# Two 384-column pieces of a selective scan joined into one of 768 columns

## The reference

```python
def step(h, xs_t):
    d_t, u_t, B_t, C_t = xs_t
    dA = jnp.exp(d_t[..., None] * A)
    h = h * dA + (d_t * u_t)[..., None] * B_t[:, :, None, :]
    y = jnp.einsum('bkdn,bkn->bkd', h, C_t)
    return (h, y)
...
x = x + _L0_conv_ref(_gn(x), ...)     # projections, 3x3 conv, the scans, gated output
x = x + _L1_conv_ref(_gn(x), ...)     # qkv, 3x3 conv, softmax(q k^T) v, projection
```

## Time and profile before

| | |
|---|---|
| time, median of 3 runs | 11736.53 us (11725.92 to 11742.42) |
| the profiled execution: its own time | 11744.59 us |
| the profiled execution: its span | 11742.8 us |
| DVE busy | 8777.8 us, 75% |
| PE busy (matmuls) | 7829.1 us, 67% |
| ACT busy | 6619.8 us, 56% |
| POOL busy | 5947.9 us, 51% |
| TensorE clock granted, mean | 0.763 of full |

### The profile page before, as it was taken

How to read it: one execution, slowest core, us unless ns; L and a number is a source line. 1 busy time by engine, 2 the same in 40 slices (tenths; PEclk the granted TensorE clock), 3 DMA queues, 4 the chain that set the end, 5 groups by cost and what they waited for, 6 DMA issues and landing times.

```text
span 11742.8 us, 196590 instructions
## 1 busy us (share of the span) xinstructions
PE 7829.1 (67%) x53104; PEld 2469.3 (21%) x53104; DVE 8777.8 (75%) x12459; ACT 6619.8 (56%) x12403; POOL 5947.9 (51%) x4844
## 2 busy tenths in 40 slices
PE   3555467873788638885487845878458774687758
PEld 1221122221222212221122211222112221222212
DVE  4998578975899649996499965989569986698740
ACT  3332366643676437763477634766257753576558
POOL 3665446644566336664266633666346654465420
PEclk7555578875888758886588866989568885798779
DMA  3554145531555225551355513554135541455310
GB/s 88 170 166 141 23 145 168 159 104 41 153 169 157 80 59 155 173 155 58 83 159 170 153 39 104 161 164 146 45 111 161 162 144 23 133 165 163 116 22 19
DMA packets 686888, 1411.01 MB, mean 120 GB/s; under 512 B 74400, under 2 KB 334272, under 8 KB 678080
## 3 DMA queue, kind: packets, MB, share of 16 engines
q1 hardware_dynamic: 686016, 1401.21, 40.0%
HBM read 1186.22 MB, written 214.70 MB: 119 GB/s over the span
## 4 chain that ended last, share of the span: by engine, by line
issue 34%; DVE 20%; POOL 19%; PE 15%; DMA 6%; ACT 4%; SPq 2%; DVEq 1%; POOLq 1%; ACTq 0%
POOL hc_buf L624 18%; DVE rings L980 11%; DVE ps L956 4%; PE ps L1347 3%; PE ps L1200 2%; DMA rep<-bc_scratch 2%; PE ps L1377 2%; PE ps L1378 2%; PE ps L1266 1%; ACT probs_buf L723 1%; DMA hc_buf<-y_scratch 1%; PE ps L1419 1%; POOL u_buf L295 1%; DVE rep L905 1%; DMA delta_scratch<-job_buf 1%
## 5 line engine op out<-in xcount | busy, mean ns | idle before, releaser
L624 POOL TENSOR_TENSOR hc_buf<-rings,rep 128x384 f32<-128x384 f32 x4608 | 4948.8, 1074 | 3713.1 <-DVE rings L980 3700.8
L723 ACT ACTIVATE probs_buf<-ps 128x384 f32<-128x384 f32 x6912 | 3081.3, 494 | 2008.1 <-PE ps L1266 1979.8
L956 DVE TENSOR_TENSOR ps<-ps,rep 128x384 f32<-128x384 f32 x4608 | 2505.8, 545 | 667.0 <-PE ps L1175 413.6
L1175 PE MATMUL ps<-st_buf,pick_channel 96*128 96x384 bf16 x4608 | 1722.7, 374 | 1531.8 <-DVE rings L980 1282.3
L1266 PE MATMUL ps<-qp_buf,kp_buf 108*128 108x384 bf16 (+1 forms) x6912 | 2224.8, 352 | 142.3 <-ACT job_buf L682 98.8
L980 DVE TENSOR_TENSOR_SCAN rings<-rings,ps 128x384 f32<-128x384 f32 x2304 | 2282.9, 991 | 9.0
L980 DVE TENSOR_TENSOR_SCAN rings<-st_buf,rings,ps 128x384 f32<-128x384 f32 x1920 | 1922.5, 1001 | 0.0
L1200 PE MATMUL ps<-probs_buf,v_buf 128*13 128x384 f32 x13824 | 1624.2, 545 | 31.8 <-ACT probs_buf L723 17.9
L1188 PE MATMUL ps<-hc_buf,sum_states 128*32 128x144 f32 x24576 | 1491.8, 330 | 86.8 <-POOL hc_buf L624 86.8
L714 ACT ACTIVATE st_buf<-st_buf,a_cols 128x768 f32<-128x768 f32 x1152 | 1076.7, 937 | 153.3 <-DMA st_buf<-delta_scratch 149.7
L1266 PEld LDWEIGHTS ps<-qp_buf,kp_buf 108*128 108x128 bf16 x6912 | 663.7, 98 | 2286.0 <-ACT probs_buf L723 1097.5
(11 more groups left out here) (147 smaller groups left out, 6751.2 us busy)
## 6 DMA issues: line engine op xcount, KB each, us to landing
st_buf<-delta_scratch SPq DMA_DIRECT2D x1152, 384.0 KB
rings<-delta_scratch SPq DMA_DIRECT2D x1152, 384.0 KB
part_scratch<-job_buf SPq DMA_DIRECT2D x1152, 72.0 KB, 2.8
st_buf<-part_scratch SPq DMA_DIRECT2D x192, 432.0 KB, 6.8
rep<-bc_scratch SPq DMA_DIRECT2D x192, 384.0 KB
delta_scratch<-job_buf SPq DMA_DIRECT2D x192, 192.0 KB, 5.2
qp_buf<-qk_scratch SPq DMA_DIRECT2D x864, 36.0 KB
kp_buf<-qk_scratch SPq DMA_DIRECT2D x432, 72.0 KB
```

What stands on the lines that cost most here:

```text
L624: pool.tensor_tensor(hc[tile % 2][:, cols], h_ring[x % 2], rep_piece(1, kk, v), ALU.mult)\
L723: act.activation(probs[(m % 2) * HG + h], bank(slots["score", p]), ACT.Exp, scale=SCALE)\
L956: dve.tensor_tensor(bu, bu, rep_piece(0, kk, v), ALU.mult)\
L1175: pe.matmul(bank(BANK_U[x % 3]), pick(x // 2), st[x // 2 // SPG][:, piece(v)], start=True, stop=True)\
```

## The change

A piece becomes a whole step of 768 columns for the broadcast, the product by B, the scan and the product by C, and the semaphores count steps in place of halves.

- PE writes a step's 768 columns with two matmuls (512 and 256 columns) into one of **two** u slots of two PSUM banks each (banks 2 to 5), one directly behind the other. Broadcast t waits for scan t-2.
- Scores, denominators, projection and jobs keep a ring of **two** banks in place of three.
- DVE's product t is followed directly by scan t, which reads it. The number of products and of scans goes from 4608 to 2304 each.
- `h_ring` becomes two slots of 768; the second lies in unused columns of `job_buf`.
- Delta loads, exp(delta A), sums over states, jobs and attention keep their size and their place. The part of attention without a scan beside it keeps its ring of 7.

```diff
-SCAN_RING = 3
+SCAN_RING = 2
...
-        h_ring = [rings[:, (6 + i) * PC:(7 + i) * PC] for i in range(2)]
+        h_ring = [rings[:, 6 * PC:8 * PC], job_buf[:, 8 * PC:10 * PC]]
...
-        BANK_U, BANK_Y, BANK_PV = (3, 4, 5), 6, 7
+        BANK_Y, BANK_PV = 6, 7
+        flat = ps[:, :, :].rearrange("p b c -> p (b c)")
+        U0 = 2 * 512
...
+        def u_slot(t, lo=0, hi=SC):
+            return flat[:, U0 + t % 2 * 1024 + lo:U0 + t % 2 * 1024 + hi]
...
-                            pool.tensor_tensor(hc[tile % 2][:, cols], h_ring[x % 2], rep_piece(1, kk, v), ALU.mult)\
-                                .then_inc(s["hc_ready"], 1)
+                            pool.tensor_tensor(hc[tile % 2][:, chunk(kk, v)], h_ring[t % 2], rep_third(1, kk, v),
+                                               ALU.mult).then_inc(s["hc_ready"], 1)
...
-                dve.wait_ge(s["ubc"], X + 1)
-                bu = bank(BANK_U[x % 3])
-                dve.tensor_tensor(bu, bu, rep_piece(0, kk, v), ALU.mult)\
+                dve.wait_ge(s["ubc"], kidx * DSTEPS + q * BODY + (t + 1))
+                dve.tensor_tensor(u_slot(t), u_slot(t), rep_third(0, kk, t % SPT), ALU.mult)\
                    .then_inc(s["b_ready"], 1)
...
-                if x % 2 == 0:
-                    dve.wait_ge(s["da_ready"], kidx * DSTEPS + q * BODY + (x // 2 + 1))
-                if not (first and x < 2):
+                dve.wait_ge(s["da_ready"], X + 1)
+                if not (first and t < 2):
 
                     dve.wait_ge(s["hc_ready"], X - 1)
-
-                if not (first and x == 0):
+                if not (first and t == 0):
                     dve.wait_ge(s["h_ready"], X)
                 dve.wait_ge(s["b_ready"], X + 1)
...
-                o, d0, d1 = h_ring[x % 2], da_ring[x // 2 % RD][:, piece(v % 2)], bank(BANK_U[x % 3])
+                o, d0, d1 = h_ring[t % 2], da_ring[t % RD], u_slot(t)
...
-                if scan:
-                    mult_b(kidx, kk, q, 0, first)
                 for t in range(BODY):
                     if scan:
-                        for x in (2 * t, 2 * t + 1):
-                            if x + 1 < 2 * BODY:
-                                mult_b(kidx, kk, q, x + 1, first)
-                            scan_half(kidx, kk, q, x, first)
+                        mult_b(kidx, kk, q, t, first)
+                        scan_chunk(kidx, kk, q, t, first)
...
-                if not (first and x < 3):
-                    pe.wait_ge(s["h_ready"], X - 2)
-                v = natural(kk, x % (2 * SPT))
-                pe.matmul(bank(BANK_U[x % 3]), pick(x // 2), st[x // 2 // SPG][:, piece(v)], start=True, stop=True)\
-                  .then_inc(s["ubc"], 1)
+                if not (first and t < 2):
+                    pe.wait_ge(s["h_ready"], X - 1)
+                src = st[t // SPG][:, chunk(kk, t % SPT)]
+                pe.matmul(u_slot(t, 0, 512), pick(t), src[:, 0:512], start=True, stop=True)
+                pe.matmul(u_slot(t, 512, SC), pick(t), src[:, 512:SC], start=True, stop=True).then_inc(s["ubc"], 1)
```

More of the change, by code:

```diff
@@ L305, in rep_third, with chunk @@
             return rep[:, slot * SC:(slot + 1) * SC]
-        def rep_piece(j, kk, v):
-            return rep_third(j, kk, v // 2)[:, piece(natural(kk, v) % 2)]
+        def chunk(kk, i):
+            cc = natural(kk, i)
+            return slice(cc * SC, (cc + 1) * SC)
+        def u_slot(t, lo=0, hi=SC):
+            return flat[:, U0 + t % 2 * 1024 + lo:U0 + t % 2 * 1024 + hi]
         loads = [(in_proj, "in_projT"), (taps[0], "taps_a"), (taps[1], "taps_b"),
@@ L612, in stretch @@
                     def stretch(q, first):
-                        for x in range(2 * BODY):
-                            X = kidx * (2 * DSTEPS) + q * (2 * BODY) + x
-                            tile, v = divmod(x, 2 * SPT)
-                            cols = piece(natural(kk, v))
-                            if first and tile == 0 and v % 2 == 0:
-                                pool.wait_ge(rep_loaded[v // 2], 32 * (kidx + 1))
+                        for t in range(BODY):
+                            X = kidx * DSTEPS + q * BODY + t
+                            tile, v = divmod(t, SPT)
+                            if first and tile == 0:
+                                pool.wait_ge(rep_loaded[v], 32 * (kidx + 1))
                             if v == 0 and not (first and tile < 2):
@@ L945, in job_stage, with mult_b, scan_chunk @@
                 ins.then_inc(s["job_dve"], 1)
[L947 to L956 removed]
+            def mult_b(kidx, kk, q, t, first):
+                if first and t < SPT:
+                    dve.wait_ge(rep_loaded[t], 32 * (kidx + 1))
+                dve.wait_ge(s["ubc"], kidx * DSTEPS + q * BODY + (t + 1))
+                dve.tensor_tensor(u_slot(t), u_slot(t), rep_third(0, kk, t % SPT), ALU.mult)\
                    .then_inc(s["b_ready"], 1)
[L959 to L961 removed]
+            def scan_chunk(kidx, kk, q, t, first):
+                X = kidx * DSTEPS + q * BODY + t
                 back = KS_ORDER[kk] >= 2
[L963 to L966 removed]
+                dve.wait_ge(s["da_ready"], X + 1)
+                if not (first and t < 2):
                     dve.wait_ge(s["hc_ready"], X - 1)
[L970 removed]
+                if not (first and t == 0):
                     dve.wait_ge(s["h_ready"], X)
@@ L973, in scan_half @@
                 init = 0.0
-                if x % (2 * SPT):
-                    prev = h_ring[(x + 1) % 2]
-                    init = prev[:, 0:1] if back else prev[:, PC - 1:PC]
-                o, d0, d1 = h_ring[x % 2], da_ring[x // 2 % RD][:, piece(v % 2)], bank(BANK_U[x % 3])
+                if t % SPT:
+                    prev = h_ring[(t + 1) % 2]
+                    init = prev[:, 0:1] if back else prev[:, SC - 1:SC]
+                o, d0, d1 = h_ring[t % 2], da_ring[t % RD], u_slot(t)
                 if back:
@@ L1287, in stretch @@
                     if scan:
-                        broadcast_u(kidx, kk, q, 2 * t, first)
+                        broadcast_u(kidx, kk, q, t, first)
                     if scan and t % SPT != 1:
@@ L1296, in stretch @@
                         score(PER_STEP * t + 1)
-                    if scan:
-                        broadcast_u(kidx, kk, q, 2 * t + 1, first)
                     if prev and t == DEN_MM:
```

30 lines of the change are left out of this document (11 added, 19 removed).

## The result

The changed kernel takes **12272.2 us** (median of 4 runs, 12261.58 to 12272.78) where the kernel before took 11735.42 us beside it (4 runs): a ratio of 1.0456, 95% interval 1.0438 to 1.0474. It is 537 us slower; 11654 us was forecast, range 11510 to 11860. The profiled execution's span is 12270.8 us, 528 us above that of before.

What follows compares the result with a forecast made beforehand. DVE was taken to set the pace wherever a scan runs. Terms +6 - 88 + 25 + 7 - 33 = -83 us from the profiled 11744.6 gave 11662, less 8 for the median: 11654 us, range 11510 to 11860.

Steps and rivals of the forecast that it cites:

- job products of over 2 us in every stretch (the port): Sign of being wrong: DVE job products lasting over 2 us in every stretch would show the port case.
- POOL, the port: DVE job products sometimes wait for POOL's longer C product at the shared port: 30 times 0.85 us, +25 us.
- the port rival: Four job products after a sum's copy, 72 stretches, all come behind the C product: 533 us, 12190 us; 6%.
- The joined step: DVE's 768-column product plus scan: 2.75 us against 2.74, scan's wait 0.09 us (bounds 0.04 to 0.16); +6 us.
- Waits for the broadcast: DVE's waits for PE's broadcast shrink by 12.6 us in each of 7 images with attention beside them: -88 us.
- step 8's wait: DVE's product of step 8 waits for the broadcast behind PE's projection; goes whole, some 6 us per image.
- Step 3's: Stall after the attention sum's copy, ended by ACT's exponential before step 3's scan; shrinks 0.56 us each, 5.6 us per image.
- End of a direction: Last sums wait for a C product ending 0.9 us later; B's load hides it in 24 of 32 directions: +7 us.
- The loop's branch: DVE stands 5.27 us behind a branch, 14 times; shorter loop body may end it: 0 to -67, taken -33 us.
- The ring of two: Rival: scores wait for exponentials, ACT falls behind, scans wait: up to 463 us, 12117 us, or 11886 in half the steps; 18%.
- The drain rule: Rival: DVE drains anyway, so a scan's wait for the product ahead costs nothing: 11260 us; 5%.
- Gains given back: Rival: stalls of steps 2 and 7 set by ACT's chain, branch stalls stay, port costs 25 us: 11736 us; 17%.

Runs made afterwards that it cites:

- e6: The kernel before, still 384-column pieces, with each scan directly behind its own product instead of the next piece's: 12839.62 us, ratio 1.094.
- e1: The kernel before with only POOL's C product widened to 768 columns, counting its semaphore by two: 11698.51 us, ratio 0.9979.
- e9: The kernel before with only the C product in 768 columns, as in e1, but counting its semaphore by one: 11695.8 us, ratio 0.9966.
- e4: The kernel before with a ring of two banks for scores, denominators, projection and jobs, nothing else: 11899.78 us, ratio 1.0156.
- e3: The changed kernel with every DVE job or leftover instruction of two SBUF inputs directly behind a scan, at most one per step: 11621.56 us, ratio 0.991.
- e11: The kernel before, C products in 384 columns, with only the new places of jobs and leftovers from e3: 11652.63 us, ratio 0.9922.
- e8: The changed kernel with each C product counting its semaphore by two instead of one, readers' waits doubled: 11863.06 us, ratio 1.0107.

## Why the prediction was wrong

The forecast's sum was -83 us; the same terms now, from the traces. The last sign of being wrong that the prediction names, "job products of over 2 us in every stretch (the port)", is the one that came.

- **POOL, the port: +25 us forecast, +639 measured.** This is the step that failed. The mechanism and its price were right: "Each would cost 0.85 us more" against 2.19 less 1.38 for one that was lost already, and 1.85 us against 1.65 to 1.85 for one newly lost. The count was not. I took the 30 of before as given, and gave the port rival 6% because "the order behind a scan's end is unchanged". It is unchanged, and so are the record starts, but what stands ahead of the scan is not: e6 turns the race by that alone. The rival had named four products per stretch at 72 stretches, 533 us; 404 are 5.6 per stretch, for it left out the second product of step 17 and the one behind the division.
- **The joined step: +6 us forecast, +133 measured.** The product's record is 0.95 us (forecast 0.94) and scan to next start 1.73 us (1.72, so two passes per column hold). The wait was mis-sized: 0.13 us, not 0.09. A step without extras is 2.805 us from scan to scan (steps 20 and 22) instead of 2.75, where before has 2.74; 2304 x 0.065 is 150 us, less the 17 us at the stretches' ends. It lies within the bounds that I had given. I had taken the wait of a scan for a scan; that of a product for a product was as near.
- **Waits for the broadcast: -88 us forecast; -152 measured for the broadcast and +81 for exp(delta A) behind it,** so -71. By steps: step 8's wait went whole, as forecast (33 us; forecast 42). Step 3's went from 163 to 64 us, but 78 us of waits of the scan, nearly all for exp(delta A), now stand in steps 2 to 5, so the stall that ACT's chain sets there shrank by 21 us where 39 were forecast. Scattered waits in other steps gave the rest. That -71 comes near -88 is partly luck.
- **The wait for B: not in the sum, -99 us.** e1 takes it to 141.6 us, e6 to 88.0: both the wide C product and the order on DVE shorten it. Part of it has only moved into the wait of the next line.
- **End of a direction: +7 us forecast, +44 measured** (128.4 less 84.5), the list has it in all 32 directions. e1, with the wide C product alone, has 116.5, so that product makes most of it; and as the wait for B behind it is 41 us shorter there, the load of B did hide most of it, as forecast.
- **The loop's branch: -33 us forecast, -67 measured.** The stall is gone from the list of waits. It stays in e6 (60.1 us) and e9 (64.8), whose loop bodies on DVE are as long as before, and in none of the runs with 768-column products. So neither the order nor the wide C product ends it; that it is the shorter body is the reading left, which no run tests alone.
- **The ring of two, 18%:** its mechanism exists (e4), and in the change I find no more of it than the 81 us above, not 232 to 463; nearly all of them stand in steps 2 to 5 and not in 15 ordinary steps.
- **The drain rule, 5%:** refuted in its consequence here. The Trainium skill (VectorE: DVE Perf Modes, "The DRAIN you can't avoid") has it that a semaphore between chained instructions costs nothing extra; e6 shows 0.22 us for each of 4608 pairs: an instruction that is not held starts 0.09 us before its forerunner's record ends, a held one 0.13 us after.
- The Trainium skill's lock (SBUF — State Buffer, "Who interferes with whom") fits all of this in its price: the second one to issue blocks until the first is through, and the loser's record is 1.38 us with a 384-column C product and 2.19 with 768. The page goes by the order of issue, which the records do not give; by their starts it is not the first that wins: in the kernel before and in e9 POOL's record starts 0.04 to 0.05 us ahead and DVE wins.

Together 133 + 639 - 71 - 99 + 44 - 67 = 579 us, where the span grew by 528. The 51 us between I have not assigned. A long product can cover a wait that would otherwise show: e3, which has none, waits 32 us more for exp(delta A) than the change. And the terms beside the port, -60 us together, are worth less than that: e3 and e11, which differ by the change and have no long product, lie only 19 us apart in span (11633.3 and 11652.1). So the 639 us of longer records cost the span some 550.

Three sums of the prediction do not come out of its own terms. The bounds of the scan's wait, -115 to +160 us about 11654, give 11539 to 11814 and not 11510 to 11790. "Gains given back" keeps +6, +25 and +7 us, which is 11774 and not 11736. And 2304 x 0.18 us below the forecast is 11239, not 11260. None of them would have held 12272.

**What stays open:** why a held scan or product lets POOL win the race behind it; the table shows that it does, not how. And why some races are lost with nothing held close ahead: 4 behind a copy and 12 in step 5 or 17 in the kernel before, 55 and 38 in e4 (in 3 of those 4 and 21 of those 55 an instruction four or five places back was held).

## What to carry to other kernels

Where DVE instructions with two SBUF inputs and POOL instructions that read SBUF are released by the same event, count the pairs and price each outcome, however rarely the bad one shows: 276 products turned for 0.065 us. Put the two-input instruction directly behind the releasing one, at most one per release: none of 864 job products was long then (e3). The new places gave 0.8% here, and no width of the pieces gave more. When an edit makes an instruction wait for the one directly ahead, price the lost overlap as well as the gap (here 0.22 us, not 0.13).

## What was not expected of the hardware

- POOL's start behind a scan depends on what its instruction counts: 0.079 us where the C product counts by one, 0.144 where it counts by two and its wait runs as an instruction of its own (change and e8, e9 and e1). It is not the count alone: 35 C products in the first image of the changed kernel count by one and start at 0.144 us.
- A scan costs 2.11 ns per column (1.73 less 0.92 us over 384 columns), twice a product's 1.04.
- In all kernels with 384-column products a stall of some 5 us stands behind the backward branch of the two-stretch loop (14 to 20 times); in those with 768-column products, whose body on DVE is shorter, it is not there at all.
